# Adding the biases of the last layer outside TensorE: expert bias as the result leaves its bank, output bias on POOL

## The reference, cut to what matters

```python
xn = _layernorm(x, axis=-1)
x = x + _L3_attn_ref(xn, W_qkv, b_qkv, W_out, b_out) \
      + _L3_ffn_ref(xn, router_w, w1, b1, w2, b2)

# attention: 16 heads of 8, causal, softmax; then
return out @ W_out + b_out

# feed-forward: 8 experts, each token uses its best two
top_k_probs, top_k_idx = jax.lax.top_k(router_probs, 2)
top_k_probs = top_k_probs / (top_k_probs.sum(axis=-1, keepdims=True) + 1e-08)
cw = (jax.nn.one_hot(top_k_idx, E) * top_k_probs[..., None]).sum(axis=1)
for e in range(E):
    h = new_gelu(x_flat @ w1[e].T + b1[e])
    out_e = h @ w2[e].T + b2[e]
    output = output + cw[:, e:e + 1] * out_e
```

## Time and profile before

| what | value |
|---|---|
| median of three runs | 2444.83 us (2441.73 to 2447.58) |
| the profiled execution, its own time | 2441.34 us |
| its span, first to last instruction | 2439.6 us |
| PE busy | 1950.5 us, 80% |
| DVE busy | 1855.0 us, 76% |
| ACT busy | 1447.1 us, 59% |
| POOL busy | 1317.7 us, 54% |
| mean granted TensorE clock | 0.904 of full |

### The profile page before, as it was taken

One profiled execution on the slowest core, in us unless ns is written; L12 is line 12 of the kernel. 1 busy time (PEld: TensorE's weight loads), 2 busy tenths in 40 slices (PEclk: granted clock), 3 DMA queues, 4 the chain that ended last, 5 costly groups with the idle time before them and its releaser, 6 DMA issues. The chain is left out here.

```text
span 2439.6 us, 32864 instructions
## 1 busy us (share of the span) xinstructions
PE 1950.5 (80%) x10212; PEld 1016.9 (42%) x10212; DVE 1855.0 (76%) x2464; ACT 1447.1 (59%) x2630; POOL 1317.7 (54%) x962
## 2 busy tenths in 40 slices
PE   6797797979797977879857989655688988988767
PEld 5233343333333333335625777532245544554312
DVE  6499999999999999878788888756455565656741
ACT  2676777767777775563546666312476567656553
POOL 5599999989898989322324545226511111112551
PEclk9899999999898988989888999755799999999976
DMA  2354444455444545300200000022212432331110
GB/s 72 98 161 138 153 144 147 151 153 164 141 141 147 156 140 157 123 27 1 85 0 1 0 0 0 6 77 78 84 55 82 122 86 67 112 100 43 42 53 17
DMA packets 150289, 214.84 MB, mean 88 GB/s; under 512 B 30970, under 2 KB 62613, under 8 KB 149525
## 3 DMA queue, kind: packets, MB, share of 16 engines
q1 hardware_dynamic: 146052, 204.72, 27.6%
q0 software_dynamic: 4096, 8.40, 1.2%
HBM read 193.91 MB, written 23.86 MB: 89 GB/s over the span
## 5 line engine op out<-in xcount | busy, mean ns | idle before, releaser
L717 PE MATMUL ps<-m_hC,ident 128*128 128x512 f32 x1024 | 510.4, 642 | 134.9 <-DVE m_hC L1005 134.9
L914 POOL TENSOR_TENSOR m_dBx<-m_du,m_rowB 128x1024 f32<-128x1024 f32 x256 | 604.0, 2390 | 8.6 <-DMA m_rowB<-bc_rows 8.3
L2773 ACT ACTIVATE a_pT<-ps 128x512 f32<-128x512 f32 (+2 forms) x640 | 320.0, 554 | 285.2 <-PE ps L2595 249.8
L2912 DVE TENSOR_REDUCE a_mx<-ps 128x2 f32<-128x1024 f32 (+2 forms) x320 | 350.6, 1117 | 174.8 <-PE ps L2573 116.0
L840 ACT ACTIVATE ps<-m_delta,m_A 128x512 f32<-128x512 f32 x512 | 339.7, 685 | 119.5 <-DVE m_h L996 118.6
L717 PEld LDWEIGHTS ps<-m_hC,ident 128*128 128x128 f32 x1024 | 201.7, 204 | 426.6 <-issue 228.9
L3060 POOL TENSOR_SCALAR_AFFINE_SELECT a_pT<-a_pT 128x512 f32<-128x512 f32 x128 | 81.6, 637 | 454.3 <-ACT a_pT L2773 452.5
L996 DVE TENSOR_TENSOR_SCAN m_h<-ps,m_carry,m_dBx 128x512 f32<-128x512 f32 x256 | 311.2, 1265 | 9.0 <-ACT ps L840 9.0
L996 DVE TENSOR_TENSOR_SCAN m_h<-ps,m_dBx 128x512 f32<-128x512 f32 x256 | 295.9, 1206 | 19.1 <-ACT ps L840 18.5
L924 POOL TENSOR_TENSOR m_hC<-m_h,m_rowC 128x1024 f32<-128x1024 f32 x80 | 194.6, 2432 | 68.0 <-DVE m_h L996 67.7
L1005 DVE TENSOR_TENSOR m_hC<-m_h,ps 128x1024 f32<-128x1024 f32 x176 | 214.9, 1221 | 21.2 <-ACT ps L850 7.2
(11 more groups left out here) (404 smaller groups left out, 3569.5 us busy)
## 6 DMA issues: line engine op xcount, KB each, us to landing
m_rowB<-bc_rows SPq DMA_DIRECT2D x256, 256.0 KB, 4.5
m_rowC<-bc_rows SPq DMA_DIRECT2D x256, 256.0 KB, 4.2
a_w<-in_L3f_w1T SPq DMA_DIRECT2D x39, 256.0 KB, 2.6
a_w<-in_L3f_w2T SPq DMA_DIRECT2D x39, 256.0 KB, 3.4
qk_parts<-a_part SPq DMA_DIRECT2D x24, 256.0 KB
expert_rows<-in_zero_rows SPq DMA_DIRECT2D x39, 128.0 KB, 2.7
a_xs<-expert_rows SPq DMA_DIRECT2D x39, 128.0 KB, 2.3
expert_out<-a_y SPq DMA_DIRECT2D x39, 128.0 KB, 3.4
```

The lines of the kernel that those rows point to most:

```text
L717: mm = pe.matmul(ps[:, bankY + c, :], k.ident[:], hC[:, n % NBUF, c, :], start=False, stop=n % NS == NS - 1)
L914: pool.tensor_tensor(dBx[:, n % NBUF], du[:, i % 2, :, chunk(i, x)], rowB[:, n % 4, :].unsqueeze(1).to_broadcast([P, HALF, CH]), ALU.mult) ...
L2773: act.activation(dst, src, ACT.Exp).then_inc(t_read, 1)
L2912: dve.tensor_reduce(mx[:, c % 2, :, es[0]:es[0] + len(es), t, x // CH], src, AX_X, ALU.max)\
```

## The change

Five things are done.

1. The expert bias: the row b2[e] of the tile's expert is loaded with the tile, repeated over all 128 partitions (a fifth DMA in `load_tile`, ahead of w2), and `down_done` becomes one `tensor_tensor` add of the bank and that row in place of the copy.
2. `load_tile(kt)` waits for DVE's reading of the bank of tile kt - 4 (`s_read`) in place of PE's finishing of it (`s_done`); the counts on `s_t` go from 4 to 5 DMAs a tile.
3. The output bias is loaded repeated over 128 partitions, and POOL adds it to the whole of `x_tm` in four instructions of 128x1024 float32 after the copy of the constants, each giving one count of the new semaphore `biased`. `residual` and `combine` on DVE wait for all four.
4. In the merge, the four transposes of `cw` (L2662), DVE's copy `cT` (L2952) and the four matmuls with `cT` (L2673) of each half are gone; the matmul with W_out starts its own sum.
5. The router's steps "hots", "picked", "cw", "cw9" are gone, and `count` waits for "cw1".

```diff
-                for dst, src in ((wo[:], ins["L3a_wout"]), (b2[0:NE], ins["L3f_b2"]),
-                                 (b2[NE:NE + 1], ins["L3a_bout"].rearrange("(a n) -> a n", a=1))):
+                for dst, src in ((bo[:], ins["L3a_bout"].partition_broadcast(P)), (wo[:], ins["L3a_wout"])):
                     sp.dma_start(dst, src).then_inc(s_o, 16)
...
                     if kt >= 4:
-                        sp.wait_ge(s_done, s_at["DOWN", kt - 4] + 1)
+                        sp.wait_ge(s_read, s_at["DOWN", kt - 4] + 1)
...
+                    sp.dma_start(b2[:, u, :], ins["L3f_b2"][ds(e, 1), :].rearrange("a d -> (a d)").partition_broadcast(P))\
+                      .then_inc(s_t[u], 16)
                     sp.dma_start(w2[:, u, :, :], ins["L3f_w2T"][:, ds(e, 1), :, :].rearrange("p a t n -> p (a t) n"))\
                       .then_inc(s_t[u], 16)
...
                     for t in range(4):
-                        pe.transpose(k.ps[:, bank, t * P:t * P + P],
-                                     att[:, bb % 2, u * 4 + t].rearrange("p g n -> p (g n)"), k.ident[:])
-                    for t in range(4):
-                        mm = pe.transpose(k.ps[0:NE + 1, bank + 1, t * P:t * P + P], R["cw"][:, bb * 8 + u * 4 + t, :],
-                                          k.ident[:])
+                        mm = pe.transpose(k.ps[:, bank, t * P:t * P + P],
+                                          att[:, bb % 2, u * 4 + t].rearrange("p g n -> p (g n)"), k.ident[:])
...
-                        pe.matmul(k.ps[:, bank, cols], cT[:, u, cols], b2[:], start=True, stop=False, skip_group_check=True)
-                        mm = pe.matmul(k.ps[:, bank, cols], aT[:, u, cols], wo[:], start=False, stop=True,
+                        mm = pe.matmul(k.ps[:, bank, cols], aT[:, u, cols], wo[:], start=True, stop=True,
                                        skip_group_check=True)
...
-                    step(VR, dve.tensor_tensor(work[:, 0], hot[:, 0], hot[:, 1], ALU.add), "hots")
-                    step(VR, dve.tensor_tensor(pr, pr, work[:, 0], ALU.mult), "picked")
-                    step(VR, dve.tensor_tensor(R["cw"][:, :, 0:NE], pr, wide8(den), ALU.mult), "cw")
-                    step(VR, dve.memset(R["cw"][:, :, NE:], 1.0), "cw9")
...
-                    dve.tensor_copy(ys[:, kt % 2].rearrange("p a d -> p (a d)"), k.ps[:, bank, 0:2 * D]).then_inc(s_read, 1)
+                    y = k.ps[:, bank, 0:2 * D].rearrange("p (a d) -> p a d", a=2)
+                    dve.tensor_tensor(ys[:, kt % 2], y, b2[:, kt % 4, :].unsqueeze(1).to_broadcast([P, 2, D]), ALU.add)\
+                       .then_inc(s_read, 1)
...
-                    dve.tensor_copy(aT[:, u, :], k.ps[:, bank, :])
-                    dve.tensor_copy(cT[:, u, :], k.ps[0:NE + 1, bank + 1, :]).then_inc(s_read, 1)
+                    dve.tensor_copy(aT[:, u, :], k.ps[:, bank, :]).then_inc(s_read, 1)
...
+                    dve.wait_ge(biased, B)
...
+                pool.wait_ge(s_o, 32)
+                for n in range(B):
+                    x = k.x_tm[:, n * 8:n * 8 + 8, :]
+                    pool.tensor_tensor(x, x, bo[:].unsqueeze(1).to_broadcast([P, 8, D]), ALU.add).then_inc(biased, 1)
```

More of the change, by code:

```diff
@@ L2352, in attn3_stage @@
         consts = xs[:, 0:2]
-        wo, b2 = sb("w_out", [P, D]), sb("b2", [NE + 1, D])
-        aT, cT = sb("aT", [P, 2, CH]), sb("cT", [NE + 1, 2, CH])
+        wo, bo, b2 = sb("w_out", [P, D]), sb("b_out", [P, D]), sb("b2", [P, 4, D])
+        aT = sb("aT", [P, 2, CH])
         w, bcol, bv = R["w"], R["bcol"], R["bv"]
@@ L2387, in attn3_stage @@
         s_out, s_seg = k.sem("s_out"), k.sem("a3_segments")
+        biased = k.sem("a3_residual_biased")
         bias_scaled, turned_one = k.sem("a3_bias_scaled"), k.sem("a3_ones_column")
@@ L2392, in attn3_stage @@
         VR = Steps(k, "dve", ["logit", "max", "less", "sum", "rsum", "prob"] + top2_names("r")
-                   + ["two", "eps", "rden", "cw0", "cw1", "hots", "picked", "cw", "cw9"])
+                   + ["two", "eps", "rden", "cw0", "cw1"])
         VS = Steps(k, "dve", ["tot", "incl", "t1", "t2", "t3", "ends", "base", "excl", "off", "pos", "mine", "slot", "int",
@@ L2510, in _ @@
                 sp.wait_ge(s_c, 64)
-                sp.wait_ge(s_o, 48)
+                sp.wait_ge(s_o, 32)
                 for u in range(4):
@@ L2514, in _ @@
                     sp.wait_ge(s_m[u], 16 * 6 * NI // 4)
-                    sp.wait_ge(s_t[u], 16 * 4 * len(range(u, NTILE, 4)))
+                    sp.wait_ge(s_t[u], 16 * 5 * len(range(u, NTILE, 4)))
                 for u in range(2):
@@ L2544, in count @@
                     bank = take_s("C")
-                    when(pe, VR, "hots")
+                    when(pe, VR, "cw1")
                     all_hot = hot.rearrange("p r t e -> p (r t e)")
@@ L2627, in turn_rows @@
                     bank = take_s("XT", kt)
-                    pe.wait_ge(s_t[kt % 4], 16 * 4 * (kt // 4 + 1))
+                    pe.wait_ge(s_t[kt % 4], 16 * 5 * (kt // 4 + 1))
                     for a in range(2):
@@ L2668, in out_project @@
                     bank = take_s("Y", bb, u)
-                    pe.wait_ge(s_o, 48)
+                    pe.wait_ge(s_o, 32)
                     pe.wait_ge(s_read, s_at["A", bb, u] + 1)
@@ L2806, in _ @@
                             for kt in tiles_of(s):
-                                act.wait_ge(s_t[kt % 4], 16 * 4 * (kt // 4 + 1))
+                                act.wait_ge(s_t[kt % 4], 16 * 5 * (kt // 4 + 1))
                                 for x in range(2):
@@ L3113, in layer3 @@
              "out_rows": dram("expert_out", (ROWS, D)), "v": sb("v", [P, NI, QT, GH, HD + 1]), "xn": sb("xn", [P, NT, D]),
-             "cw": sb("cw", [P, NT, NE + 1]), "cwr": sb("cwr", [P, 2, NT]),
+             "cwr": sb("cwr", [P, 2, NT]),
              "slot": sb("slot", [P, 2 * NT], mybir.dt.uint32), "expert": sb("expert", [P, NTILE], mybir.dt.int32),
```

## The result

The changed kernel takes 2430.36 us, median of 4 runs (2426.68 to 2432.71), against 2446.2 (2441.73 to 2448.0, 4 runs) for the kernel before: ratio 0.9939, 95% interval 0.9917 to 0.996. Timed again at another time, the two side by side on one chip, it took 2413.52 us (6 runs) against 2434.45 (11 runs): ratio 0.9921, interval 0.9903 to 0.9939. The kernel before alone differs by about 12 us between the two, so from here on ratios are compared, or times that were taken together. The change saves 16 to 21 us; 23.3 were forecast. The 2430.36 us lie outside the forecast's own range of 2416 to 2426, and just inside its wider one of 2413 to 2431.

A forecast was written before the change was run, and what follows sets the result against it. PE was taken as the bound in the last layer's expert and merge slots. Gains of 16.3 + 9.5 less 0.5 and 2.0 made 23.3 us, so 2444.8 became 2421.5 us; own range 2416 to 2426, 8 in 10 within 2413 to 2431.

The forecast's parts named there:

- the fifth load and the moved wait: Expert tiles: the first tile loses 0.5 us; stores issued 0.95 us later make DVE wait, 0 to 8 us, taken 2.
- The merges: Slots 6, 10 and 14: PE's removed work gains 5.5, 5.5 and 5.3 us, 16.3 in all.
- The share of 5/6: Merges: five sixths of PE's added or lost time shows in the end, giving 4.8 us a merge as lower bound.
- The pitch: Output projection: matmuls of like row count stand 0.25 us apart in place of 0.416, 0.47 at half clock.
- only what is removed counts: Rival, 20%: output projection keeps pitches 0.416 and 0.72 us, so 17.5 us are gained, time 2427.3.
- The tail: Slot 18, at half clock: the shorter projection and earlier copy of aT gain 9.5 us.
- The first tile: First expert tile: PE waits for w2, which goes out one issue later, costing 0.5 us.
- The router and POOL: Start of the last layer: removed router steps gain nothing; POOL's four adds, 9.5 us, lie in idle time.
- The add in place of the copy: Expert tiles on DVE: the add takes 0.42 us, as the copy; bounds 0 to 2 us in all.
- the stores become a new wait: Rival, 16%: each of six slots loses 1.4 us waiting for stores, 8.4 in all, time 2427.9.
- Slower: Case, 3%: the repeated row slows queues, every tile's store lands late in nine slots; loss about 30 us, time 2449.
- the change hides nowhere: Rival, 2%: PE was not the bound in the merges, only the tail gains, time 2437.8.

The follow-up runs named there:

- experiment 4: The kernel before, with `b2` and `cT` zero-padded from 9 to 128 rows and all instructions kept: 2427.43 us, ratio 0.9927.
- Experiments 9 to 11: Changed kernel, stores ahead of loads: DVE's add repeated four times in slots 7, 8, 11, 2411.93 us; in slots 4, 5, 9, 2411.61; no repeats, 2401.17.
- second group: Four kernels run together on one chip with the kernel before, which took 2434.45 us there; the changed kernel, unchanged, took 2413.52 us.
- experiments 5 and 6: The changed kernel once more, 2413.52 us; the same with eight bias-row buffers and SP waiting for PE's finishing (`s_done`) again, 2406.29 us.
- experiments 1, 7 and 11: The changed kernel with each tile's store issued ahead of the loads for tile kt + 4, in three groups: 2421.5, 2405.99 and 2401.17 us.
- experiment 8: The changed kernel without POOL's four adds, the last layer's output bias left out: 2415.44 us, against 2413.52 for the changed kernel beside it.

## Why the prediction was right and wrong

The direction, the mechanism of the gain and most terms were right; one term, "the fifth load and the moved wait", called "the price", was mis-sized by a factor of about four, and it put the time outside the forecast's own range.

- **The merges: 14.7 us measured for 16.3.** Slots 6, 10 and 14 of the profiled executions went from 52.45, 52.45 and 39.33 us to 47.58, 47.65 and 34.27. PE's saving came as worked out (5.79 of 5.74 us in slot 6). Less of it reached the end than 5.5 us, since PE waits longer at other places: 0.76 us for ACT's `exps` at 1924.28 in place of 0.33, and twice 0.42 for DVE's maxima in place of 0.17. The share of 5/6, read from what the merge had added, gave 4.8 and was the better number; I should have left it there.
- **The pitch.** 0.25 us a matmul at full clock and 0.47 at half, both as taken from the like run. The rival "only what is removed counts" is excluded by this and by experiment 4.
- **The tail: 9.5 us, as worked out.** From the first transposes to DVE's last add 5.75 us, before 15.26.
- **The first tile: 0.5 us taken, 1.2 measured.** PE waits 4.17 us for w2 in place of 3.94, but it also gets there later. From the end of POOL's last scatter to PE's first transposes of the tile it is 8.1 us, before 6.9. In the ten profiles with the row it is 8.0 to 8.6, in the three without it 6.9 to 7.1. 0.5 us is the fifth issue; the rest is w2, which lands after 3.7 us in place of 3.0.

```profile
1747.01 0.97 POOL L3074 DMA_INDIRECT expert_rows<-l_xn,l_slot  x1 [0.17 <-issue]
...
1751.74 0.97 POOL L3075 DMA_INDIRECT expert_rows<-l_xn,l_slot  x1 [0.17 <-issue]
...
1760.83 0.66 PE L2632 MATMUL ps<-ident,a_xs 128*128 128x128 f32 x2 [4.17 <-DMA a_w<-in_L3f_w2T]
```

- **The router and POOL.** Nothing, as forecast. POOL's first scatter is at 1645.07, not at 1641.42, but DVE's router starts 3.6 us later too, ahead of anything that the adds could delay. Of DVE's slack of 9.3 us the adds used 3.6 (last section); I had named this cover without a size for what it had to hide.
- **The add in place of the copy.** 0.424 us, as the copy's 0.42. Nothing.
- **The fifth load and the moved wait: 2 us taken, 7 to 9 measured.** This is the step that failed, in three places. First, the delay: it was taken as 0.95 us, but over the six slots named the store goes out 1.3 us later in the mean. Second, the landing: "3.3 to 3.5 is the usual landing", and 0.3 for the row, holds in four of the six slots, but in slot 8 it is 5.6. It is not w2 as such, which stood right ahead of the store before the change too. The second store of each slot, whose buffer the fourth tile needs, in us:

| slot | 4 | 5 | 7 | 8 | 9 | 11 |
|---|---|---|---|---|---|---|
| from its issue until the fourth tile's copy could start, PE's result being there, before | 4.7 | 4.4 | 4.35 | 4.7 | 3.8 | 4.5 |
| the same for the add, after | 3.3 | 3.4 | 3.6 | 3.3 | 2.5 | 2.3 |
| its landing, before | 3.3 | 3.4 | 4.2 | 3.6 | 2.9 | 3.4 |
| its landing, after | 3.3 | 3.5 | 3.9 | 5.6 | 3.0 | 3.3 |
| the add waits beyond the usual 1.51 | 0.1 | 0.2 | 0.4 | 2.4 | 0.6 | 1.1 |

  With 0.3 in slot 10 that is 5.0 us. In slot 11 the landing is the usual one; there the issue of the row's load itself took 1.36 us, where it took 0.33 in slot 8, and held up the store behind it:

```profile
2185.91 1.36 SPq L2475 DMA_DIRECT2D a_b<-in_L3f_b  x1
...
2187.80 0.42 SPq L2483 DMA_DIRECT2D expert_out<-a_y  x1
...
2191.20 0.42 DVE L2940 TENSOR_TENSOR a_y<-ps,a_b 128x256 f32<-128x256 f32 x1 [2.60 <-DMA expert_out<-a_y]
```

  Third, I priced a wait at its own length. Experiments 9 to 11 show that a pause of PE of 1.6 us costs 3.5, because a stretch at half clock follows it. In the second group the whole step costs 7.2 us (experiments 5 and 6).
- **The rival "the stores become a new wait"** (16%) had the mechanism, and for the six slots of its list 8.4 us; the measured sum is near that, with the waits mostly in three or four slots, and the clock in it. Its 1.4 us a slot is more than its tightest row gives, 0.95 + 0.3 - 0.15 = 1.1. Its figure, 2427.9, is nearer to the measured 2430.4 than the forecast. "Slower" and "the change hides nowhere" are excluded.

The sum with the measured terms, 8 being the middle of 7 to 9: 14.7 + 9.5 - 1.2 - 8 = 15 us, against 15.8 between the medians. Without the late stores it would be 23, and experiments 1, 7 and 11 show 22.1, 28.5 and 30.3 in their three groups; the 5 to 7 us more in two of them stay unexplained. That kernel, the changed one with the store ahead of the loads, beats both kernels: 7.5 us, 0.3%, under the changed one where both ran together (2405.99 and 2413.52 us), and 1.0 to 1.3% under the kernel before.

One thing stays open: why half clock followed the waits of the same slots (7, 8 and 11) in three profiles, when six slots have the same order of work. In slots 7 and 8 the store lands late (3.9 to 5.8 us in the three profiles), in slot 11 it goes out late; what else uses the queues then was not separated.

## What to carry to other kernels

When a transfer's issue moves later in its queue, read the slack at every place where somebody waits, not at one (2.3 to 3.6 us here after the change), and compare it with the slowest landing, not the median one. Expect that landing to lengthen if bytes are put ahead of it: here from 4.2 to 5.8 us. Where PE is the bound and runs at full clock, a wait can cost twice its length, since a stretch at 1.2 GHz can follow: here 3.5 us for each one that made PE's idle time 2.7 us in place of 1.1. Before removing matmuls of few rows from between 128-row ones, try padding them to 128 rows: here that alone saved 16 us. Put the issue that somebody waits for soon ahead of the issues for half a slot later: here two exchanged lines are worth 7 us.

## What the hardware showed that was not expected

**A short idle time of PE brings half clock.** In three profiles of kernels with late stores (the changed kernel twice, experiment 8), slots 8, 9 and 12 began with PE idle 1.3 to 3.4 us and had 0.72 or less in their first 6 us; idle times of 1.51 and 1.60 us ahead of slot 10 and 1.19 ahead of slot 11 had 1.00 behind them, so length alone does not decide at that size. In the eight profiles with neither a pause nor an add that waits over 0.1 us for a store, all starts of slots 5 to 13 have 1.12 us and 1.00. The Trainium skill ("TensorE: Matmul & The Clock Gate", What's actually happening) says that the clock gate goes by how busy PE has been recently; the experiments agree in direction.

**A matmul whose row count differs from the last one's is dearer than a full one.** 9 and 128 rows in turn stand 0.416 us apart, 128 and 128 rows 0.22 (experiment 4). The weight loads (PEld) show where the time goes. In the kernel before each starts together with its own matmul; in experiment 4 it starts 0.11 us ahead of it, beside the matmul before (1937.05, shown there):

```profile
1934.20 0.30 PEld L2674 LDWEIGHTS ps<-a_w_out,a_aT 128*128 128x128 f32 x2
1934.20 0.49 PE L2674 MATMUL ps<-a_w_out,a_aT 128*128 128x128 f32 x2
...
1936.94 0.30 PEld L2676 LDWEIGHTS ps<-a_w_out,a_aT 128*128 128x128 f32 x2
```

**POOL's adds hold up DVE's operations on two SBUF tiles.** POOL's four adds run from 1603.47 for 9.63 us, so one ends at about 1605.9, 1608.3, 1610.7 and 1613.1. DVE beside them, in the changed kernel:

```profile
1603.47 9.63 POOL L3034 TENSOR_TENSOR x_tm<-x_tm,a_b_out 128x1024 f32<-128x1024 f32 x4
...
1606.16 0.42 DVE L2851 TENSOR_REDUCE a_h<-a_h 128x32 f32<-128x256 f32 x1
1606.62 1.81 DVE L2852 TENSOR_TENSOR a_h<-a_h 128x256 f32<-128x256 f32 x1
1609.83 1.08 DVE L2856 TENSOR_TENSOR a_h<-a_h 128x256 f32<-128x256 f32 x1
...
1611.40 1.99 DVE L1049 TENSOR_TENSOR a_h<-a_h 128x256 f32<-128x256 f32 x1
...
1628.48 2.01 DVE L2906 TENSOR_REDUCE a_mx<-ps 128x4 f32<-128x512 f32 x2 [7.98 <-PE ps L2575]
```

The three adds and products of two tiles take 1.81, 1.08 and 1.99 us where each took 0.43 without POOL (0.42 in experiment 8), and end at 1608.4, 1610.9 and 1613.4, just behind an end of POOL's; the reduction of one tile keeps its 0.42. Here it costs nothing, since DVE is idle for 8 us afterwards. The Trainium skill ("SBUF — State Buffer", SBUF: two separate sides) says that whichever of a DVE operation with two SBUF inputs and a GpSimd operation that reads SBUF starts first holds the shared port pair for its whole length while the other is blocked. The trace agrees, with the ends above.
